# The MLP's gated product split between ScalarE and GpSimd, and VectorE's top-k steps in another order

## The chip, the core and the metric

The kernel runs on one core of one Trainium2 chip. The metric is the device time of one execution in microseconds, the median of several runs.

## What is computed

The input x is 4 batches of 1024 tokens by 256 channels, with a context of 64 tokens and a condition vector for each batch. All of it is float32. Two layers are applied one after the other. The first has three sub-layers, each a layer norm with a scale and shift from the condition, a body, and a gated residual:

```python
h = _ln(x) * (1 + sc_msa) + sh_msa;  h = _self_attn(h, ...);        x = x + h * g_msa
h = _ln(x) * (1 + sc_mca) + sh_mca;  h = _topk_cross_attn(h, ...);  x = x + h * g_mca
h = _ln(x) * (1 + sc_mlp) + sh_mlp;  h = _swiglu(h, ...);           x = x + h * g_mlp

def _swiglu(h, w_m1, b_m1, w_m2, b_m2):
    u = h @ w_m1 + b_m1                     # 256 -> 2048
    a, b = (u[..., :HID], u[..., HID:])     # HID = 1024
    return jax.nn.silu(a) * b @ w_m2 + b_m2
```

The self attention has 16 heads of 16 channels in windows of 128 tokens. The first cross attention keeps for each token and head the 16 largest of 64 scores. The second layer is a plain cross attention with a residual. The change touches how `silu(a) * b` is formed and when the steps of the top 16 run.

## The kernel before

**Blocks and layers.** The 4096 tokens go through in 8 blocks of 512 (two for each batch), each with W = 4 tiles or windows of 128. The code numbers the bodies: layer 1 is the self attention, 2 the top-k cross attention, 3 the MLP, 4 the last cross attention. Work is pipelined over blocks. After `first()` and `second()`, a call `full(a)` for a = 2 to 7 does layer 1 of block a, the scores and the top-k of layer 2 of block c = a - 1, and the rest of layer 2 and layers 3 and 4 of block b = a - 2. `last()` does what is left of blocks 6 and 7, so that it holds two MLPs, and nothing of layer 1. Every engine has its own `full(a)` and `last()`, an order written out by hand; an engine's queue is strictly in this order.

**Banks.** TensorE's results go through the 8 PSUM banks in turn, in the order of `bank_order()`. A result is a key such as ("ua", n, j); TensorE waits until the bank's last user has drained it (`fill_wait`), readers wait until it is filled (`filled_wait`), and the last read is marked with `drain`. So each result needs the one that was 8 places earlier to be read.

**The MLP.** `mlp_in(n)` forms for each of J = 8 chunks j of 128 channels two results of 128x512: "ua" (to be gated by silu) and "ub" (the linear half), six matmuls each: float32 inputs are split in a rounded part and a rest (`qr` and `h_low`; `w_m1` and `m1_low`). Before, ScalarE's `silu(n, j)` (L800 to L805) reads "ua" and writes `sa[:, j % 2, :]`, a buffer of two, which is the tile `rden`. VectorE's `gated_linear(n, j)` (L1074 to L1080) adds the bias to "ub", multiplies by `sa` and writes `hid[:, j, :]` (in the tile `arena`), in one instruction at L1079. `project(3, n)` on TensorE waits until "ub" of chunk 7 is drained and multiplies `hid` by `w_m2`: 64 matmuls, the second MLP product.

**The top-k.** `topk(n, t, steps)` on VectorE (L1042 to L1063) has five steps for a tile t. Steps 0 and 2 find eight maxima of each of 16 heads (L1060), steps 1 and 3 take them out of the scores (L1062), step 4 multiplies the exponentials by the mask (L1054, 128x1024, with two operands in SBUF, `left` and `eS`). Between them GpSimd's `subtract_max(n, t)` (L626 to L631, waits for step 0 of its tile and for step 4 of the tile before) writes `eS`, and ScalarE's `topk_exp(n, t)` (L770) exponentiates it; step 4 waits for that. TensorE's `probs(n)` transposes the result a block later. Exponentials and silu need different tables on ScalarE, so `topk_exp(c, 1)`, which stands in the MLP loop after chunk 3, has a table load on each side.

**Self attention around it.** For window w TensorE forms scores "A" for the maxima. VectorE's `window_max(n, w)` (L1021 to L1026) reduces four banks; TensorE transposes the maxima ("mT") and forms the scores "B" minus the maxima; ScalarE exponentiates them, TensorE forms the values "PV", ScalarE's `self_denominator` (L741 to L750) the reciprocals, and VectorE's `window_divide` (L1028 to L1032) the quotient. In the order of banks the four "B" of window 2 take over the banks of "PV" of window 0 and of the first three "A" of window 3. In `full(a)` before, VectorE runs between `window_max(a, 2)` and `window_max(a, 3)`:

```python
window_max(a, 2)
normalise(4, b, (3, b))
topk(c, 3, (0,))
window_divide(a, 0)
window_max(a, 3)
topk(c, 3, (1,))
```

**GpSimd** has otherwise the reciprocal square roots (`layer_rstd`), the sums `add_bias` (L614) and the scaling of weights by the gates (`gate_weight`, L622). SyncE issues all DMAs.

Of the kernel before, what the change touches and what calls it, by code (L numbers as in the profile page):

```python
# [12 lines left out]
P = 128  # L13
# [12 lines left out]
BT = W * P  # L26
# [221 lines left out]
def build(nc, t_in, out):  # L248
    ctx = ExitStack()
    with ctx:  # L250
# [60 lines left out]
        rden_self = sb("rden_self", [P, 2, KC * P])  # L311
        top = sb("top", [P, H, TOPK])
# [94 lines left out]
        s_rd = [sem(f"cross_denominators{n}") for n in range(5)]  # L407
        s_top8 = sem("top8_done")
# [186 lines left out]
        def _(pool):  # L595
# [29 lines left out]

            def subtract_max(n, t):  # L626
# [29 lines left out]
            for a in range(2, BLOCKS):  # L656
# [7 lines left out]
                if a % BLKS:  # L664
                    gate_weight(1, batch)
                else:
                    gate_weight(0, batch)
                subtract_max(c, 1)
                subtract_max(c, 2)
                layer_rstd(4, b)  # L670
# [10 lines left out]
            add_bias(3, b)  # L681
            subtract_max(c, 1)
            subtract_max(c, 2)
# [4 lines left out]
            add_bias(3, c)  # L688
            layer_rstd(4, c)
# [3 lines left out]
        def _(act):  # L693
# [106 lines left out]
            def silu(n, j):  # L800
                if j >= 2:
                    drained_wait(act, ("ub", n, j - 2))
                key = ("ua", n, j)
                filled_wait(act, key)
                drain(nc.scalar.activation(sa[:, j % 2, :], ps(key), ACT.Silu, bias=chan[:, CB["m1"] + j:CB["m1"] + j + 1]), key)  # L805

# [148 lines left out]
        def _(dve):  # L955
# [118 lines left out]
            def gated_linear(n, j):  # L1074
                drained_wait(dve, ("ua", n, j))
                key = ("ub", n, j)
                filled_wait(dve, key)
                at = CB["m1"] + J + j
                drain(nc.vector.scalar_tensor_tensor(hid[:, j, :], ps(key), chan[:, at:at + 1], sa[:, j % 2, :],  # L1079
                                                     ALU.add, ALU.mult), key)  # L1080

# [144 lines left out]
            def full(a):  # L1226
# [11 lines left out]
                for j in range(J):  # L1238
                    gated_linear(b, j)
                    if j < 5:  # L1240
                        topk(c, 1, (j,))
                    elif j == 5:
                        topk(c, 2, (0,))
                window_max(a, 0)
                window_max(a, 1)
                topk(c, 2, (1, 2))
                residual_moments(3, b, (0,))
                topk(c, 2, (3, 4))
# [3 lines left out]
                topk(c, 3, (0,))  # L1252
                window_divide(a, 0)
                window_max(a, 3)
                topk(c, 3, (1,))
# [12 lines left out]
            def last():  # L1268
# [7 lines left out]
                for j in range(J):  # L1276
                    gated_linear(b, j)
                    if j < 5:
                        topk(c, 1, (j,))
# [520 lines left out]
```

## Time and profile before

| | before |
|---|---|
| median of 3 runs | 1036.91 us (1036.07 to 1039.96) |
| the profiled execution | 1035.79 us, span 1033.6 us |
| TensorE matmul busy | 897.5 us, 87% |
| VectorE busy | 750.6 us, 73%, 3953 instructions |
| ScalarE busy | 475.0 us, 46%, 792 instructions |
| GpSimd busy | 219.1 us, 21%, 162 instructions |
| the chain that ended last | TensorE 58%, VectorE 30%, ScalarE 6%, issue 5% |

Busy time is the time in which an engine has an instruction under way. The chain is followed back from the last instruction, at each step to what released it; "issue" is time in which the engine waited for nothing that the profile shows. TensorE's granted clock, PEclk, is a share of full speed: 1.00 is 2.4 GHz, 0.50 is 1.2 GHz. In the tables below PE is TensorE, DVE is VectorE, ACT is ScalarE and POOL is GpSimd; L1314 and the like are lines of the kernel before. Ends of matmuls are modelled, and all matmuls of one helper share its line, L1314.

### The profile page before, as it was taken

The page shows a single profiled execution, that of the slowest core. Times are in us where ns is not written, and L with a number is a line of the kernel's source. Part 1 is how long each engine was busy: PE and PEld are TensorE (multiplying, and loading weights), DVE is VectorE, ACT ScalarE, POOL GpSimd, SP SyncE. Part 2 cuts the span into 40 slices and gives each one's busy share as a digit, 9 for nine tenths or more (in the row PEclk, how much of TensorE's full clock was granted, in tenths as well). Part 3 has the DMA queues.
Part 4 walks back from the last instruction along what each step waited for, and adds up shares of the span by engine and source line. Part 5 has one row for each costly group of instructions (what it writes and reads, how often), then busy time and mean ns, then how long its engine had stood idle before and what let it go on. Part 6 is the DMA issues. An engine that isn't in the chain of part 4 may idle for free.

```text
span 1033.6 us, 22090 instructions
## 1 busy us (share of the span) xinstructions
PE 897.5 (87%) x8088; PEld 653.4 (63%) x8088; DVE 750.6 (73%) x3953; ACT 475.0 (46%) x792; POOL 219.1 (21%) x162
## 2 busy tenths in 40 slices
PE   6977656998999989998999899998999898767975
PEld 4744543786567756875678656775678566644763
DVE  3647866897579957997589757996599758875322
ACT  3336333625564356526463557426562554315313
POOL 1025411402041404211140404120230303120010
PEclk9988777999999999999999999999999998888999
DMA  8250010000100102000100111000100110000000
GB/s 326 98 168 11 2 42 1 17 2 3 41 17 1 53 18 62 11 2 2 57 2 1 53 50 35 7 2 1 57 2 11 43 31 1 2 1 1 21 1 21
DMA packets 29051, 32.96 MB, mean 32 GB/s; under 512 B 4320, under 2 KB 26000, under 8 KB 28688
## 3 DMA queue, kind: packets, MB, share of 16 engines
q1 hardware_dynamic: 28944, 31.55, 9.4%
q8 instruction: 65, 1.06, 0.4%
q14 instruction: 42, 0.34, 0.1%
HBM read 25.19 MB, written 6.36 MB: 31 GB/s over the span
## 4 chain that ended last, share of the span: by engine, by line
PE 58%; DVE 30%; ACT 6%; issue 5%; DMA 1%; POOL 1%; SPq 0%; DVEq 0%; ACTq 0%; POOLq 0%
PE bank L1314 52%; DVE left L1062 8%; DVE top L1060 6%; DVE negm L1025 3%; DVE arena L1079 3%; PE bank L1481 3%; DVE negm L1087 2%; PE bank L1332 2%; ACT arena L816 2%; DVE arena L1054 1%; DVE xh L973 1%; DVE h_low L1072 1%; ACT hT L705 1%; DVE vpad L1016 1%; DMA w_m<-in_w_ada 1%
## 5 line engine op out<-in xcount | busy, mean ns | idle before, releaser
L1314 PE MATMUL bank<-w_m,arena 128*128 128x256 f32 x512 | 115.2, 387 | 6.1 <-issue 6.1
L601 POOL TENSOR_SCALAR veps<-mv 128x4 f32<-128x4 f32 (+1 forms) x33 | 8.1, 245 | 499.8 <-DVE mv L968 499.7
L1314 PEld LDWEIGHTS bank<-w_m,arena 128*128 128x128 f32 x512 | 98.8, 194 | 20.9 <-issue 6.9
L630 POOL TENSOR_TENSOR eS<-arena,top 128x1024 f32<-128x1024 f32 x32 | 61.9, 1935 | 206.8 <-DVE top L1060 206.7
L1062 DVE MATCH_REPLACE8 left<-top,arena 128x64 f32<-128x64 f32 x512 | 99.8, 208 | 0.0
L1062 DVE MATCH_REPLACE8 left<-top,left 128x64 f32<-128x64 f32 x512 | 99.8, 207 | 0.0
L759 ACT ACTIVATE arena<-bank 128x512 f32<-128x512 f32 x128 | 66.1, 603 | 55.3 <-PE bank L1314 55.3
L805 ACT ACTIVATE rden<-bank,chan 128x512 f32<-128x512 f32 x64 | 44.0, 688 | 102.7 <-PE bank L1314 76.8
L1314 PE MATMUL bank<-qr,w_m 128*128 128x512 f32 x256 | 82.3, 402 | 3.9 <-ACT qr L715 3.2
L1314 PE MATMUL bank<-qr,m_low 128*128 128x512 f32 x256 | 80.4, 396 | 0.0
L1025 DVE TENSOR_REDUCE negm<-bank 128x4 f32<-128x512 f32 x128 | 78.6, 680 | 2.0 <-PE bank L1314 1.9
L1060 DVE MAX8 top<-arena 128x8 f32<-128x64 f32 x512 | 67.7, 209 | 16.2 <-ACT arena L779 16.2
L1314 PE MATMUL bank<-h_low,w_m 128*128 128x512 f32 x256 | 70.3, 396 | 0.5 <-DVE h_low L1072 0.5
L1060 DVE MAX8 top<-left 128x8 f32<-128x64 f32 x512 | 67.8, 209 | 0.5
L999 DVE TENSOR_TENSOR x<-bank,x 128x512 f32<-128x512 f32 x48 | 33.0, 688 | 40.7 <-PE bank L1314 40.7
L724 ACT ACTIVATE qk<-bank,chan 128x512 f32<-128x512 f32 x48 | 33.0, 687 | 63.3 <-PE bank L1314 63.3
L1314 PE MATMUL bank<-q_by_parity,qk 32*128 32x256 f32 x512 | 38.3, 414 | 23.6 <-DVE negm L1025 13.0
L1314 PEld LDWEIGHTS bank<-qr,w_m 128*128 128x128 f32 x256 | 48.6, 191 | 15.8 <-issue 3.6
L1314 PE MATMUL bank<-hT,w_qkv 128*128 128x512 f32 x128 | 58.0, 607 | 0.2 <-ACT hT L705 0.2
L1079 DVE SCALAR_TENSOR_TENSOR arena<-bank,chan,rden 128x512 f32<-128x512 f32 x64 | 46.8, 741 | 15.4 <-ACT rden L805 15.4
L1314 PEld LDWEIGHTS bank<-h_low,w_m 128*128 128x128 f32 x256 | 48.5, 190 | 11.9 <-DVE h_low L1072 1.5
L788 ACT ACTIVATE arena<-bank 128x512 f32<-128x512 f32 x64 | 32.4, 633 | 50.1 <-PE bank L1481 50.1
(133 smaller groups left out, 1840.7 us busy)
## 6 DMA issues: line engine op xcount, KB each, us to landing
w_m<-in_w_m SPq DMA_DIRECT2D x4, 1024.0 KB, 5.5
xin<-in_x SPq DMA_DIRECT2D x4, 512.0 KB, 3.9
arena<-in_w_m SPq DMA_DIRECT2D x1, 2048.0 KB, 12.4
out<-x SPq DMA_DIRECT2D x4, 512.0 KB, 2.9
arena<-in_w_ada SPq DMA_DIRECT2D x1, 1536.0 KB, 10.8
gate<-gate_rows SPq DMA_DIRECT2D x12, 128.0 KB, 3.6
gated_bias<-gate_rows SPq DMA_DIRECT2D x12, 128.0 KB, 3.8
xin<-in_x SPq DMA_DIRECT2D x4, 384.0 KB, 3.1
```

The costliest lines, as they stand in the source:

```text
L630: nc.gpsimd.tensor_tensor(eS[:], S[:, t, :].rearrange("p (h n) -> p h n", h=H), top[:, :, 0:1].to_broadcast([P, H, LC]), ALU.subtract).the ...
L724: drain(nc.scalar.activation(dst, ps(key), ACT.Identity, bias=chan[:, n:n + 1]), key)
L759: drain(nc.scalar.activation(pT_self[:, w % 2, 4 * r:4 * r + 4, :], ps(key).rearrange("p (h q) -> p h q", h=4), ACT.Exp, scale=SCORE_SCALE ...
L788: drain(nc.scalar.activation(pT[:, 4 * k:4 * k + 4, t * P:(t + 1) * P], ps(key).rearrange("p (h q) -> p h q", h=4), ACT.Copy), key)
L805: drain(nc.scalar.activation(sa[:, j % 2, :], ps(key), ACT.Silu, bias=chan[:, CB["m1"] + j:CB["m1"] + j + 1]), key)
L999: drain(nc.vector.tensor_tensor(x[:, slot, tiles], ps(key).rearrange("p (t n) -> p t n", t=2), src, ALU.add), key)
L1025: drain(nc.vector.tensor_reduce(negm[:, w, r, 0:4], ps(key).rearrange("p (h n) -> p h n", h=4), AX_X, ALU.max, negate=True), key)
L1060: i = nc.vector.max(eight, scores)
L1062: i = nc.vector.match_replace(left[:, h, :], eight, scores, REPLACED)
L1079: drain(nc.vector.scalar_tensor_tensor(hid[:, j, :], ps(key), chan[:, at:at + 1], sa[:, j % 2, :], ALU.add, ALU.mult), key)
L1314: return nc.tensor.matmul(dst, lhsT, rhs, start=start, stop=stop)
L1481: i = nc.tensor.transpose(ps(key)[:, p * P:(p + 1) * P], S[:, t, at:at + P], ident[:])
```

## The change

ScalarE's `silu(n, j)` has a second instruction, which copies "ub" with its bias into a new buffer of two, `linear`, and drains it. GpSimd's new `gated(n, first, end)` waits for both and multiplies `sa` and `linear` into `hid`, counted by the new semaphore `s_hid`. `silu` waits for the product two chunks back by `s_hid`, and so does `project(3, n)` for all eight. `gated_linear` goes from VectorE. The products stand in GpSimd's queue around the `subtract_max` of tiles 1 and 2. On VectorE five steps of tile 1 and three of tile 2 run between the last steps of tile 0 and `window_max(a, 0)`, where the gated products and six steps were. Later steps move forward by one or two places. In `last()` it is alike.

```diff
--- before.py
+++ after.py
@@ -309,6 +309,7 @@
         mTs3 = sb("mTs3", [P, BT], F32R)
         rden = sb("rden", [P, 2, BT])
         rden_self = sb("rden_self", [P, 2, KC * P])
+        linear = sb("linear", [P, 2, BT])
         top = sb("top", [P, H, TOPK])
         left = sb("left", [P, H, LC])
         eS = sb("eS", [P, H, LC])
@@ -405,6 +406,7 @@
         s_xb = [sem(f"bias{n}_added") for n in range(5)]
         s_rd1 = sem("self_denominators")
         s_rd = [sem(f"cross_denominators{n}") for n in range(5)]
+        s_hid = sem("mlp_product_done")
         s_top8 = sem("top8_done")
         s_dif = sem("max_subtracted")
         s_exp = sem("topk_exp_done")
@@ -623,6 +625,13 @@
                                                 gate[:].unsqueeze(1).to_broadcast([P, KC, C]), ALU.mult)
                 i.then_inc(s_gated[layer], 1)
 
+            def gated(n, first, end):
+
+                for j in range(first, end):
+                    drained_wait(pool, ("ua", n, j))
+                    drained_wait(pool, ("ub", n, j))
+                    nc.gpsimd.tensor_tensor(hid[:, j, :], sa[:, j % 2, :], linear[:, j % 2, :], ALU.mult).then_inc(s_hid, 1)
+
             def subtract_max(n, t):
                 pool.wait_ge(s_top8, n * W + t + 1)
                 if n + t:
@@ -665,8 +674,11 @@
                     gate_weight(1, batch)
                 else:
                     gate_weight(0, batch)
+                gated(b, 0, 2)
                 subtract_max(c, 1)
+                gated(b, 2, 7)
                 subtract_max(c, 2)
+                gated(b, 7, J)
                 layer_rstd(4, b)
                 add_bias(4, b)
                 subtract_max(c, 3)
@@ -679,13 +691,16 @@
             add_bias(2, c)
             subtract_max(c, 0)
             add_bias(3, b)
+            gated(b, 0, 2)
             subtract_max(c, 1)
+            gated(b, 2, J)
             subtract_max(c, 2)
             layer_rstd(4, b)
             add_bias(4, b)
             subtract_max(c, 3)
             layer_rstd(3, c)
             add_bias(3, c)
+            gated(c, 0, J)
             layer_rstd(4, c)
             add_bias(4, c)
 
@@ -799,10 +814,13 @@
 
             def silu(n, j):
                 if j >= 2:
-                    drained_wait(act, ("ub", n, j - 2))
+                    act.wait_ge(s_hid, n * J + j - 1)
                 key = ("ua", n, j)
                 filled_wait(act, key)
                 drain(nc.scalar.activation(sa[:, j % 2, :], ps(key), ACT.Silu, bias=chan[:, CB["m1"] + j:CB["m1"] + j + 1]), key)
+                key, at = ("ub", n, j), CB["m1"] + J + j
+                filled_wait(act, key)
+                drain(nc.scalar.activation(linear[:, j % 2, :], ps(key), ACT.Identity, bias=chan[:, at:at + 1]), key)
 
             def last_exps(n):
                 pT = probs_of(4, n)
@@ -1070,14 +1088,6 @@
                 for k in range(KC):
                     drained_wait(dve, ("T", 3, n, k))
                     nc.vector.tensor_tensor(h_low[:, k, :], h3T[:, k, :], qr[:, k, :], ALU.subtract).then_inc(s_h_low, 1)
-
-            def gated_linear(n, j):
-                drained_wait(dve, ("ua", n, j))
-                key = ("ub", n, j)
-                filled_wait(dve, key)
-                at = CB["m1"] + J + j
-                drain(nc.vector.scalar_tensor_tensor(hid[:, j, :], ps(key), chan[:, at:at + 1], sa[:, j % 2, :],
-                                                     ALU.add, ALU.mult), key)
 
             def last_max(n):
                 for u in range(2):
@@ -1235,24 +1245,19 @@
                 input_rest(b)
                 take_values(a, 1)
                 topk(c, 0, (3, 4))
-                for j in range(J):
-                    gated_linear(b, j)
-                    if j < 5:
-                        topk(c, 1, (j,))
-                    elif j == 5:
-                        topk(c, 2, (0,))
+                topk(c, 1, (0, 1, 2, 3, 4))
+                topk(c, 2, (0, 1, 2))
                 window_max(a, 0)
                 window_max(a, 1)
-                topk(c, 2, (1, 2))
+                topk(c, 2, (3, 4))
                 residual_moments(3, b, (0,))
-                topk(c, 2, (3, 4))
+                topk(c, 3, (0,))
                 residual_moments(3, b, (1,))
                 window_max(a, 2)
                 normalise(4, b, (3, b))
-                topk(c, 3, (0,))
                 window_divide(a, 0)
+                topk(c, 3, (1,))
                 window_max(a, 3)
-                topk(c, 3, (1,))
                 window_divide(a, 1)
                 last_max(b)
                 topk(c, 3, (2,))
@@ -1273,19 +1278,17 @@
                 topk(c, 0, (0,))
                 input_rest(b)
                 topk(c, 0, (1, 2, 3, 4))
-                for j in range(J):
-                    gated_linear(b, j)
-                    if j < 5:
-                        topk(c, 1, (j,))
-                topk(c, 2, (0, 1))
+                topk(c, 1, (0, 1, 2, 3, 4))
+                topk(c, 2, (0, 1, 2, 3))
                 residual_moments(3, b, (0,))
-                topk(c, 2, (2, 3, 4))
+                topk(c, 2, (4,))
+                topk(c, 3, (0,))
                 residual_moments(3, b, (1,))
-                topk(c, 3, (0,))
+                topk(c, 3, (1,))
                 normalise(4, b, (3, b))
-                topk(c, 3, (1,))
+                topk(c, 3, (2,))
                 last_max(b)
-                topk(c, 3, (2, 3, 4))
+                topk(c, 3, (3, 4))
                 cross_divide(2, c)
                 residual_moments(2, c)
                 cross_divide(4, b)
@@ -1293,8 +1296,6 @@
                 residual(4, b, 0)
                 residual(4, b, 1)
                 input_rest(c)
-                for j in range(J):
-                    gated_linear(c, j)
                 residual_moments(3, c)
                 normalise(4, c, (3, c))
                 last_max(c)
@@ -1422,7 +1423,7 @@
                 if layer == 1:
                     drained_wait(pe, ("PV", n, W - 1))
                 elif layer == 3:
-                    drained_wait(pe, ("ub", n, J - 1))
+                    pe.wait_ge(s_hid, (n + 1) * J)
                 else:
                     drained_wait(pe, ("O", layer, n, KC - 1))
                 for u in range(2):
```

## Rows read from the trace of the kernel before

**Rows 1.** Busy us by stretch (PE, PEld, DVE, ACT, POOL, clock), a = 4.

```profile
390.00:503.00 113.00, 105.93 (x995) 78.20 (x993) 91.17 (x492) 58.25 (x98) 23.39 (x17) 1.00 0.07 20
```

**Rows 2.** TensorE in time, a = 4: start us, us, [idle before <-releaser].

```profile
443.25 1.17 PE L1314 MATMUL bank<-qk,q_by_parity 32*128 32x128 f32 x32 [1.04 <-DVE arena L1079]
...
444.35 14.08 PE L1314 MATMUL bank<-w_m,arena 128*128 128x256 f32 x64
...
469.13 1.10 PE L1314 MATMUL bank<-q_by_parity,qk 32*128 32x256 f32 x13 [1.13 <-DVE negm L1025]
```

**Rows 3.** The chain that ended last: start us, us; three blocks.

```profile
388.12 3.49 PE bank L1481 x32
...
501.09 3.49 PE bank L1481 x32
...
615.19 3.49 PE bank L1481 x32
```

**Rows 4.** Costliest groups: xcount | busy us, mean ns | idle before.

```profile
L630 POOL TENSOR_TENSOR eS<-arena,top 128x1024 f32<-128x1024 f32 x32 | 61.9, 1935 | 206.8 <-DVE top L1060 206.7
...
L1079 DVE SCALAR_TENSOR_TENSOR arena<-bank,chan,rden 128x512 f32<-128x512 f32 x64 | 46.8, 741 | 15.4 <-ACT rden L805 15.4
...
L805 ACT ACTIVATE rden<-bank,chan 128x512 f32<-128x512 f32 x64 | 44.0, 688 | 102.7 <-PE bank L1314 76.8 <-DVE arena L1079 25.8
...
L622 POOL TENSOR_TENSOR w_m<-w_m,gate 128x512 f32<-128x512 f32 x16 | 19.8, 1274 | 0.0
```

**Rows 5.** VectorE in order of time, MLP loop of a = 4.

```profile
423.19 1.23 DVE L1054 SCALAR_TENSOR_TENSOR arena<-left,eS 128x1024 f32<-128x1024 f32 x1
...
424.99 2.11 DVE L1060 MAX8 top<-arena 128x8 f32<-128x64 f32 x16
...
427.02 0.73 DVE L1079 SCALAR_TENSOR_TENSOR arena<-bank,chan,rden 128x512 f32<-128x512 f32 x1
...
430.78 0.74 DVE L1079 SCALAR_TENSOR_TENSOR arena<-bank,chan,rden 128x512 f32<-128x512 f32 x1
...
443.01 4.87 DVE L1025 TENSOR_REDUCE negm<-bank 128x4 f32<-128x512 f32 x8
```

**Rows 6.** ScalarE in order of time, a = 4.

```profile
438.00 0.69 ACT L805 ACTIVATE rden<-bank,chan 128x512 f32<-128x512 f32 x1 [2.06 <-DVE arena L1079]
...
440.75 0.69 ACT L805 ACTIVATE rden<-bank,chan 128x512 f32<-128x512 f32 x1 [2.06 <-PE bank L1314]
...
466.25 0.42 ACT L750 ACTIVATE rden_self<-rden_self 128x256 f32<-128x256 f32 x1
```

**Rows 7.** Two lines of VectorE: duration ns min/median/max.

```profile
L1054 DVE SCALAR_TENSOR_TENSOR arena<-left,eS x32: 1209/1225/1274, 102.4 to 936.5; 128x1024 f32<-128x1024 f32 x32
...
L1072 DVE TENSOR_TENSOR h_low<-xh,qr x16: 680/684/2861, 192.2 to 962.8; 128x512 fp32r<-128x512 f32 x16
```

**Rows 8.** GpSimd in order of time, last stage: a bias sum.

```profile
865.51 2.83 POOL L614 TENSOR_TENSOR x<-x,gated_bias 128x1024 f32<-128x1024 f32 x1
```

**Rows 9.** VectorE in order of time, windows 2, 3 of a = 4.

```profile
461.06 2.48 DVE L1025 TENSOR_REDUCE negm<-bank 128x4 f32<-128x512 f32 x4 [0.25 <-PE bank L1314]
...
463.46 1.37 DVE L973 TENSOR_SCALAR xh<-x,mv,rstd 128x256 f32<-128x256 f32 x4
...
466.79 0.40 DVE L1031 TENSOR_TENSOR oT_self<-bank,rden_self 128x256 f32<-128x256 f32 x1
...
467.11 2.47 DVE L1025 TENSOR_REDUCE negm<-bank 128x4 f32<-128x512 f32 x4
```

**Rows 10.** TensorE in order of time, last stage.

```profile
895.59 16.66 PE L1314 MATMUL bank<-w_m,arena 128*128 128x256 f32 x64 [4.91 <-issue]
...
917.84 2.21 PE L1332 MATMUL bank<-ident,xh 128*128 128x128 f32 x8 [5.59 <-DVE xh L973]
...
984.90 14.05 PE L1314 MATMUL bank<-w_m,arena 128*128 128x256 f32 x64 [1.21 <-issue]
```

**Rows 11.** Busy us and granted clock of a stretch, last stage.

```profile
895.00:897.00 2.00, 1.41 (x3) 1.18 (x4) 2.00 (x14) 1.01 (x1) 0.00 (x0) 0.50 0.00 0
```

## The prediction

> **What bounds the kernel now.** I read the busy time by stage first. In one of the six middle blocks, a = 4, TensorE is busy 105.9 of 113 us and VectorE 91.2; ScalarE has 58.3 and GpSimd 23.4 [rows 1]. So TensorE bounds the middle, and VectorE can only cost time where TensorE stands still for it. Next I read where it stands still [rows 2]: 1.04 us before the second window's scores, where it waits for the last gated product to drain its bank, and 1.13 us before the third window's scores B(a, 2), where it waits for the fourth window's maxima. From 444.35 the second MLP product runs without a hole. The chain of waits passes the block's first transposes every 112.97 us (388.12 to 501.09), and once after 114.10 (501.09 to 615.19) [rows 3]; nothing in a block runs to a clock other than TensorE's own, so what TensorE loses at one place is not given back behind it. Only the last stage, from 842 us on, is sparse enough for VectorE to lead.
>
> **Part 1, the product leaves VectorE.** Removed: 64 gated products of 741 ns, issued 0.65 us apart. Added: 64 ScalarE copies out of PSUM, priced like the silu of the same shape, 688 ns, and 64 GpSimd products. Of those no row exists. Nearest is GpSimd's 128x512 product in place, 1274 ns; its subtraction over 128x1024 takes 1935 ns, which halved gives 0.97, the other end [rows 4]. I take 1.27, the row with the same shape and operation. Per pair of products TensorE needs 2.75 us (438.00 to 440.75 between two silus [rows 6]), ScalarE will need 1.38 and GpSimd 1.27, so neither becomes the bound inside the loop.
>
> VectorE does not get free by it before the maxima. From 423.19 to 443.01 it works without idling [rows 5]. Out go 8 x 0.65 = 5.2 us. In come two top-k steps that used to follow the maxima, tile 2's steps 1 and 2: 3.11 us (430.78 - 427.02 - 0.65) and 2.03 us (427.02 - 424.99), together 5.14. Window 0's maxima start at 443.0 as before.
>
> **Part 2, the lock between VectorE and GpSimd.** New in the change is that GpSimd reads and writes SBUF while VectorE runs step 4 of tile 0 (L1054, two SBUF inputs). So far L1054 never met a GpSimd instruction: its 32 times lie within 1209 to 1274 ns. Another two-input instruction did: L1072 takes 684 ns as a rule and 2861 at worst [rows 7], and that one ran while GpSimd's bias sum was at work from 865.51, itself 2.83 long [rows 8]. The product of j = 0 starts when silu and copy of j = 0 are done, 440.75 - 7 x 2.75 + 0.69 + 0.69 = 422.9, and ends at 424.1 or 424.2; L1054 would start at 423.19 and is held until then, some 0.95 us. Ends: 0 if there is no lock, 1.27 for a whole product. The Trainium skill's "SBUF — State Buffer", section "Who interferes with whom", says that a VectorE instruction with two SBUF inputs and a GpSimd instruction that reads SBUF exclude each other for their full length, while one with a single SBUF input doesn't contend. By that rule the sum has +2.1 us in the next part, without it -1.8.
>
> **Part 3, when the second MLP product starts.** ScalarE finishes the last copy at 440.75 + 1.38 = 442.1 [rows 6], so the second window's scores start some 1.0 us earlier. But the second product now waits for GpSimd: product 6 ends at 438.00 + 1.38 + 1.27 = 440.65, then `subtract_max(c, 2)` stands ahead of product 7 (1.94, to 442.6), then product 7 ends at 443.9. It waits too for the bank of window 0's first maxima, 443.0 + 0.6 = 443.6, with the lock 444.6. Start: 444.0 without the lock, 444.7 with it, against 444.35 [rows 2]: -0.3 or +0.35. I take +0.35, since a two-input row shows the lock: 6 x 0.35 = **+2.1 us**.
>
> **Part 4, the new order of the top-k steps.** This is the largest term. VectorE's work around the fourth window was: maxima of window 2 at 461.06, normalising at 463.46, step 0 of tile 3, division of window 0 at 466.79, maxima of window 3 at 467.11 [rows 9]. The division cannot start before ScalarE's reciprocal is done, 466.25 + 0.42 = 466.67 [rows 6]; step 0 just filled the wait. In the new order step 0 has gone ahead of `residual_moments(3, b, (1,))`, where VectorE has the time. The wait before the division stays empty, though (from the end of the normalising, about 464.8, to 466.7), and step 1, 3.11 us, stands between the division and window 3's maxima. So these start 3.05 us later (3.11 less the 0.06 that the division gains). TensorE needs three of their four banks for B(a, 2), and its queue is in order: last query, values of window 1 and the maxima of layer 4 all stand behind. Its wait goes from 1.13 to 4.2 us. Before, step 1 lay behind the maxima, in a hole in which VectorE waited for TensorE anyway. Price: 6 x 3.05 = **+18.3 us**; ends 2.9 and 3.2 each, since start times move by 0.1.
>
> **Part 5, the clock.** TensorE's granted clock is 1.00 in this block [rows 1]. In the last stage, after 4.91 us of idleness before 895.59, it stands at 0.50 [rows 11], the 1.2 GHz level, and the same 64 matmuls take 16.66 us instead of the 14.05 that they take after 1.21 us of idleness: 2.6 us lost [rows 10]. The block of 114.10 us had one fall without a long wait, 1.1 us lost [rows 3]. A wait of 4.2 us with little work ahead of it lies near the first. I take a fall in five blocks of six at 1.6 us, between 1.1 and 2.6 and nearer the lower since few dense matmuls follow it at once: **+8 us**. Ends: 0 (it never falls) and 6 x 2.6 = 15.6.
>
> **Part 6, the last stage.** In the first of its two MLP products VectorE is behind: TensorE ends at 890.68, the second product starts at 895.59. GpSimd and ScalarE will follow TensorE by 0.69 + 0.27 (the copy has to wait for its silu) + 1.27, so it starts near 893.0. From its end to the next transposes there are 5.59 us now [rows 10]; VectorE comes 1.2 us less late, and step 1 in place of step 0 costs 1.1 more, so 5.4. Transposes: 893.0 + 14.05 + 5.4 = 912.4 against 917.84, a gain of 5.4; if the clock falls in the wait of 2.3 us as well, 2.8. I take the middle, **-4.1 us**. Of the very last MLP product nothing covers the tail: before 984.90 stands a wait of 1.21 for one gated product; now copy and product, one after the other, make it 2.5: **+1.3 us**, with a fall of the clock 3.9. SP's queue moves nowhere; no DMA is added. On GpSimd `layer_rstd(4, b)` stands behind product 7, but the moments it works on come only after the second MLP product's 14 us, so it waits for nothing new.
>
> **Sum.** 2.1 + 18.3 + 8 - 4.1 + 1.3 = +25.6 us on the profiled execution's own 1035.8, so 1061.4 us. The median of the runs shown is 1.1 above the profiled one; a tenth of a per cent.
>
> **Rivals.** (a) *The clock holds* in the waits of 4.2 us. For it: waits around 1 us never lower it. Against: the fall after 4.91 us. Time: 1035.8 + 2.1 + 18.3 - 5.4 + 1.3 = 1052. Chance 0.25. (b) *The clock falls each time* for the full 2.6 and also at the last product: 1035.8 + 2.1 + 18.3 + 15.6 - 2.8 + 3.9 = 1073. Chance 0.15. (c) *Faster: the fourth window's maxima are off the path.* Place: the wait before B(a, 2). If the bank that TensorE waits for there were another's, or if VectorE reached step 1 over 3 us earlier (reciprocal before 464), the 18.3 and the 8 would go, and without the lock the earlier start of part 3 counts: 1035.8 - 1.8 - 5.4 + 1.3 = 1030. It decides for it if window 3's maxima start by 467.2 in this block's time. Against it: TensorE resumes at 469.13, right behind the third of the four maxima, the last that B(a, 2) needs (467.11, 0.6 each). Chance 0.06. (d) *The change doesn't do what it says*: GpSimd, waiting in its queue for the top-k's `s_top8`, holds back silu through the two-deep buffer and so TensorE, inside the loop. In the middle blocks this doesn't reach TensorE: the subtraction of tile 1 ends about 429.3, and the silu that needs product 2 comes at 432 or later. If a whole 1.94 were lost per block on top: 1061.4 + 11.6 = 1073. Chance 0.05. The forecast itself, with a fall in most blocks: 0.49.
>
> **Numbers.** Low: rival (a) with 2.9 for 3.05 and without the lock, 1052 - 0.9 - 3.9 = 1047. High: rivals (b) and (d), 1073. The three runs shown lie 3.9 us apart, so each end moves out by 3, to 1044 and 1076. Outside lie (c) and what (b) and (d) bring together. A measurement of this kernel tells about 0.5% (5 us) from no change. Slower by over 0.5%: forecast, (a), (b), (d), 0.94, less 0.03 for terms that cancel. Faster 0.05, same 0.04, slower 0.91.
>
> **What the profile of after would show.** Right, if TensorE's first B(a, 2) matmul has some 4.2 us of idleness released by L1025, once in each of six blocks, if VectorE idles about 2 us before the division of window 0, if the chain passes a block in 116 to 119 us, and if the clock shows 0.5 shortly after those waits. The lock would show as L1054 at 2 us or so in one of four, the others at 1.23. The second product should start within 0.5 us of where it did. Wrong, if window 3's maxima follow the division at once, if the clock stays 1.00, or if the silus in a middle block space out beyond 2.75 us.

## The result and the profile after

| | before | after |
|---|---|---|
| median | 1036.66 us of 4 runs (1036.07 to 1039.96) | 1074.31 us of 4 runs (1072.76 to 1075.02) |
| the profiled execution | 1035.79 us, span 1033.6 us | 1075.02 us, span 1072.7 us |
| ratio of the medians | | 1.0354, 95% interval 1.033 to 1.0379 |

The changed kernel is 3.5% slower. The forecast was 1061.4 us in a range of 1044 to 1076. So the direction and the range held, and the size came out 13 us short: +25.6 us forecast, +37.7 us by the medians, +39.2 us between the two profiled executions (+39.1 by their spans, which the accounts below use).

First the page of after: the span, the busy time of each engine, and two of the costliest groups (busy us, mean ns | idle before, releaser).

```profile
span 1072.7 us, 22154 instructions
...
PE 912.5 (85%) x8088; PEld 661.4 (62%) x8088; DVE 717.4 (67%) x3889; ACT 511.9 (48%) x856; POOL 307.8 (29%) x226
...
L633 POOL TENSOR_TENSOR arena<-rden,linear 128x512 f32<-128x512 f32 x64 | 89.2, 1399 | 95.0 <-ACT linear L823 93.8
...
L1315 PE MATMUL bank<-q_by_parity,qk 32*128 32x256 f32 x512 | 44.2, 466 | 42.6 <-DVE negm L1043 31.4
```

The totals say that the change did what it was written for: VectorE has 33 us less to do (750.6 before), ScalarE 37 and GpSimd 89 more, and none of the three is near the span. They don't say why the time rose. That stands in the last row: TensorE waited 31.4 us before the scores B for VectorE's maxima. The same row of the page of before has 13.0:

```profile
L1314 PE MATMUL bank<-q_by_parity,qk 32*128 32x256 f32 x512 | 38.3, 414 | 23.6 <-DVE negm L1025 13.0
```

TensorE's matmuls are the same, and yet take 15 us more (897.5 before). Their mean granted clock is 0.944 where it was 0.960.

Next the chain of waits in after, at the first transposes of three middle blocks.

```profile
283.58 3.49 PE bank L1482 x32
...
402.88 3.49 PE bank L1482 x32
...
522.27 3.49 PE bank L1482 x32
```

A block takes 119.3 to 119.5 us; it took 112.97 [rows 3]. Now TensorE in order of time in after: block a = 4 (402.88 here is 388.12 before, so 14.76 is to be taken off), then the last stage.

```profile
455.81 2.29 PE L1315 MATMUL bank<-qk,q_by_parity 32*128 32x128 f32 x64
...
460.12 14.05 PE L1315 MATMUL bank<-w_m,arena 128*128 128x256 f32 x64 [2.02 <-DVE negm L1043]
...
487.90 2.09 PE L1315 MATMUL bank<-q_by_parity,qk 32*128 32x256 f32 x16 [4.16 <-DVE negm L1043]
...
490.67 4.81 PE L1315 MATMUL bank<-hT,w_last 128*128 128x512 f32 x8
...
933.55 15.59 PE L1315 MATMUL bank<-w_m,arena 128*128 128x256 f32 x64 [2.43 <-issue]
...
954.61 2.21 PE L1333 MATMUL bank<-ident,xh 128*128 128x128 f32 x8 [5.47 <-DVE xh L991]
956.83 5.54 PE L1315 MATMUL bank<-hT,w_last 128*128 128x512 f32 x8
...
1023.99 14.05 PE L1315 MATMUL bank<-w_m,arena 128*128 128x256 f32 x64 [2.41 <-issue]
```

The second product starts at 445.36 in before's time, 1.0 us late against [rows 2]. B(a, 2) starts at 473.14, 4.0 us late, after a wait of 4.16 us where it was 1.13. Its own 16 matmuls then take 2.09 us and not 1.10. The block gains 6.42 us in all, so another 2.4 us come in behind the wait. The windows of 2 us around it show from what (PE, PEld, DVE, ACT, POOL busy, then the granted clock):

```profile
484.00:486.00 2.00, 0.00 (x0) 0.00 (x0) 2.00 (x22) 0.85 (x3) 0.84 (x1) 1.00 0.00 0
486.00:488.00 2.00, 0.10 (x4) 0.13 (x4) 2.00 (x4) 0.00 (x0) 0.00 (x0) 0.53 0.00 0
488.00:490.00 2.00, 2.00 (x24) 1.81 (x26) 0.35 (x1) 0.00 (x0) 0.00 (x0) 0.50 0.00 0
490.00:492.00 2.00, 2.00 (x18) 1.36 (x15) 0.00 (x0) 1.27 (x3) 0.00 (x0) 0.50 0.00 0
492.00:494.00 2.00, 2.00 (x4) 0.74 (x4) 0.00 (x0) 0.79 (x2) 0.00 (x0) 0.77 0.00 0
```

The clock goes to half (1.2 GHz) within the wait, some 1.8 us before B starts, and TensorE's first 5 us of work behind it run at that level.

VectorE in order of time in after, the same block and one row of the last stage:

```profile
437.95 2.08 DVE L1072 SCALAR_TENSOR_TENSOR arena<-left,eS 128x1024 f32<-128x1024 f32 x1
...
439.96 2.10 DVE L1078 MAX8 top<-arena 128x8 f32<-128x64 f32 x16
...
445.33 2.12 DVE L1078 MAX8 top<-left 128x8 f32<-128x64 f32 x16
...
459.30 4.86 DVE L1043 TENSOR_REDUCE negm<-bank 128x4 f32<-128x512 f32 x8
...
482.44 0.42 DVE L1049 TENSOR_TENSOR oT_self<-bank,rden_self 128x256 f32<-128x256 f32 x1 [1.95 <-ACT rden_self L765]
...
485.89 2.47 DVE L1043 TENSOR_REDUCE negm<-bank 128x4 f32<-128x512 f32 x4
...
929.73 2.33 DVE L1072 SCALAR_TENSOR_TENSOR arena<-left,eS 128x1024 f32<-128x1024 f32 x1
```

The division waits 1.95 us, which step 0 of tile 3 used to fill, and step 1 fills the 3.03 us between its end and window 3's maxima. In [rows 9] these begin 0.3 us after the division begins. GpSimd in the same block:

```profile
437.64 1.31 POOL L633 TENSOR_TENSOR arena<-rden,linear 128x512 f32<-128x512 f32 x1 [5.96 <-ACT linear L823]
...
454.57 1.32 POOL L633 TENSOR_TENSOR arena<-rden,linear 128x512 f32<-128x512 f32 x1 [0.16 <-ACT linear L823]
455.85 1.93 POOL L639 TENSOR_TENSOR eS<-arena,top 128x1024 f32<-128x1024 f32 x1
457.74 1.29 POOL L633 TENSOR_TENSOR arena<-rden,linear 128x512 f32<-128x512 f32 x1
```

The first product ends at 438.95, and step 4, started by the profile at 437.95, comes out at 2.08 us where it took 1.23 [rows 5].

The account of the spans' 39.1 us: the six middle blocks +40.0, the start -0.7, the last stage -0.2. In the blocks, 18.5 us of added wait before B (3.03 to 3.20 each), six times 1.0 at the second product (6.0), 14.2 of half clock behind B (some 2.4 each), one more fall in a second product of 15.69 us (1.6), less the fall of 1.1 us that before had in one block. The last 0.8 is not explained; it lies in the first of the six blocks, whose second product came 2.15 us late and not 1.0.

### The profile page after: what moved, and what is told of

Read it like the earlier page. It is cut to its first block, busy times and chain, and to the rows that moved or that the text cites. A ratio compares the mean times of both kernels' runs of the same rounds, so it can differ in the third digit from the quotient of the medians.

```text
span 1072.7 us, 22154 instructions
## 1 busy us (share of the span) xinstructions
PE 912.5 (85%) x8088; PEld 661.4 (62%) x8088; DVE 717.4 (67%) x3889; ACT 511.9 (48%) x856; POOL 307.8 (29%) x226
## 4 chain that ended last, share of the span: by engine, by line
PE 58%; DVE 28%; ACT 8%; issue 3%; DMA 1%; POOL 1%; SPq 0%; DVEq 0%; ACTq 0%; POOLq 0%
PE bank L1315 54%; DVE left L1080 11%; DVE top L1078 6%; ACT arena L774 2%; DVE negm L1043 2%; PE bank L1482 2%; DVE negm L1097 2%; DVE arena L1072 2%; PE bank L1333 2%; ACT arena L834 2%; ACT hT L720 1%; DVE h_low L1090 1%; DVE vpad L1034 1%; DVE oT_self L1049 1%; ACT rden_self L765 1%
## 5 line engine op out<-in xcount | busy, mean ns | idle before, releaser
L633 POOL TENSOR_TENSOR arena<-rden,linear 128x512 f32<-128x512 f32 x64 | 89.2, 1399 | 95.0 <-ACT linear L823 93.8
L774 ACT ACTIVATE arena<-bank 128x512 f32<-128x512 f32 x128 | 66.1, 602 | 81.7 <-PE bank L1315 81.7
L1049 DVE TENSOR_TENSOR oT_self<-bank,rden_self 128x256 f32<-128x256 f32 x32 | 13.4, 419 | 103.0 <-ACT rden_self L765 103.0
L1315 PE MATMUL bank<-q_by_parity,qk 32*128 32x256 f32 x512 | 44.2, 466 | 42.6 <-DVE negm L1043 31.4
L770 ACT ACTIVATE mTs<-bank 128x128 fp32r<-128x128 f32 x32 | 9.0, 282 | 106.4 <-PE bank L1384 106.4
L1315 PEld LDWEIGHTS bank<-q_by_parity,qk 32*128 32x128 f32 x512 | 28.5, 218 | 49.7 <-issue 48.3
```

The lines of the kernel that those rows point to most:

```text
L633: nc.gpsimd.tensor_tensor(hid[:, j, :], sa[:, j % 2, :], linear[:, j % 2, :], ALU.mult).then_inc(s_hid, 1)
L774: drain(nc.scalar.activation(pT_self[:, w % 2, 4 * r:4 * r + 4, :], ps(key).rearrange("p (h q) -> p h q", h=4), ACT.Exp, scale=SCORE_SCALE ...
L1049: drain(nc.vector.tensor_tensor(oT_self[:, :, w * P:(w + 1) * P], ps(key)[:, 0:KC * P].rearrange("p (c n) -> p c n", c=KC), rden_self[:, w ...
L1315: return nc.tensor.matmul(dst, lhsT, rhs, start=start, stop=stop)
```

## The experiments

Theory T: the position of step 1 ahead of window 3's maxima costs most, directly and through the clock. Rivals: the split itself, or the lock between VectorE and GpSimd. Each ratio is against runs of the kernel before on the same chip; their medians were 1037.36, 1040.52, 1040.34 and 1040.40 us in the four groups.

**The maxima first.** The changed kernel with one pair of lines in their old order.

```diff
                 window_divide(a, 0)
-                topk(c, 3, (1,))
                 window_max(a, 3)
+                topk(c, 3, (1,))
```

> The kernel after, with one exchange in full(a) on VectorE: the fourth window's maxima run ahead of step 1 of tile 3 again; the product split and all else stay. Theory (the order is the cost): TensorE's wait before B(a, 2) falls from 4.16 to about 1.1 us and the clock no longer falls there, so six times 3.0 + 2.4 = 32.6 us come back and the time is about 1042. Rival (the split itself is the cost, through ScalarE, GpSimd or the lock): the time stays above 1065.

1047.29 us (1045.53 to 1048.61), ratio 1.0096 (1.0068 to 1.0124). Against the changed kernel 27 us are back, from one line. TensorE in time:

```profile
334.96 15.64 PE L1315 MATMUL bank<-w_m,arena 128*128 128x256 f32 x64 [2.04 <-DVE negm L1043]
...
361.23 1.10 PE L1315 MATMUL bank<-q_by_parity,qk 32*128 32x256 f32 x13 [1.03 <-DVE negm L1043]
```

The wait before B is 1.03 to 1.07 in all six blocks. What stays are the waits of 2.04 us before the second product, and in this block the clock was low behind it (15.64 for 14.05). That happened in two of the six blocks. In three blocks the clock also fell some 43 us after the second product's start, at the scores of the last layer, for 1.1 us each; before had one such fall (its block of 114.10). Blocks take 113.9 to 116.7 us. The expectation was 5 us low for these falls, which come to 6.5 us where the changed kernel had one of 1.6 outside the place before B.

**The split alone.** The changed kernel with all of VectorE's top-k steps where they stood before, less the gated products.

```diff
-                topk(c, 2, (0, 1, 2))
+                topk(c, 2, (0,))
                 window_max(a, 0)
                 window_max(a, 1)
-                topk(c, 2, (3, 4))
+                topk(c, 2, (1, 2))
                 residual_moments(3, b, (0,))
-                topk(c, 3, (0,))
+                topk(c, 2, (3, 4))
                 residual_moments(3, b, (1,))
                 window_max(a, 2)
                 normalise(4, b, (3, b))
+                topk(c, 3, (0,))
                 window_divide(a, 0)
-                topk(c, 3, (1,))
                 window_max(a, 3)
+                topk(c, 3, (1,))
```

The steps of the last stage go back in the same way.

> The kernel after, but VectorE runs the order of the kernel before with the gated products left out (five steps of tile 1 and one of tile 2, then the maxima, and so on; last() alike). Theory: window 0's maxima come 5 us earlier and no longer hold the second MLP product; it starts when GpSimd's last product is done, which is where it started before. Middle blocks 113.0 us as before, the last stage 0 to 3 us shorter: 1034 to 1037. Rival (the split costs by itself): above 1042.

1037.79 us (1035.01 to 1039.64), ratio 0.9999 (0.9986 to 1.0013): no difference. TensorE in time:

```profile
331.44 14.05 PE L1315 MATMUL bank<-w_m,arena 128*128 128x256 f32 x64 [1.03 <-issue]
...
356.13 1.10 PE L1315 MATMUL bank<-q_by_parity,qk 32*128 32x256 f32 x13 [0.86 <-DVE negm L1043]
```

Moving the product costs nothing and brings nothing. VectorE stands idle for 3.0 us ahead of the first maxima, and TensorE now waits 1.03 us for GpSimd's product 7, behind the subtraction. All the loss lies in the order of VectorE's steps, or in that order together with the split.

**The order alone.** The kernel before, gated products on VectorE, with one pair of lines swapped.

```diff
                 window_divide(a, 0)
-                window_max(a, 3)
                 topk(c, 3, (1,))
+                window_max(a, 3)
```

> The kernel before, gated product on VectorE, with one exchange in full(a): step 1 of tile 3 ahead of the fourth window's maxima. Theory: TensorE waits 4.2 us before B(a, 2) and its clock falls each time; six times 3.1 + 2.4 = 33 us on top of before, about 1070. Rival (the step costs only together with the split): within 5 us of before, 1037 to 1042. If only the wait and not the clock counts: 1055.

1072.55 us (1071.31 to 1074.69), ratio 1.0341 (1.0315 to 1.0366). TensorE in time:

```profile
485.89 2.09 PE L1314 MATMUL bank<-q_by_parity,qk 32*128 32x256 f32 x16 [4.22 <-DVE negm L1025]
```

The wait is 4.22, 3.61, 4.22, 4.22, 4.21 and 4.17 us in the six blocks. One swapped pair of lines in the kernel before gives nearly the whole loss of the change. Blocks take 117.7 to 119.4 us: some 3.1 us of added wait cost 4.7 to 6.4, on average 5.8.

**The lock taken away.** The changed kernel, with GpSimd's first product held until step 4 of tile 0 is over.

```diff
+                pool.wait_ge(s_prob, c * W + 1)
                 gated(b, 0, 2)
```

> The kernel after, with a wait on GpSimd ahead of the first two products in full(a) until step 4 of tile 0 is done, so that the two no longer meet. Theory (lock): VectorE's step 4 of tile 0 goes from 2.08 back to 1.23 us, window 0's maxima and with them the second MLP product start 0.85 us earlier, six times: 1069. Rival (the 2.08 us have another reason): the step still takes 2.08 and the time stays at 1074. If the later products hold ScalarE back: above 1075.

1073.18 us (1072.80 to 1074.32), ratio 1.0346 (1.0324 to 1.0369); the changed kernel stands at 1074.31. VectorE, then TensorE, in time:

```profile
435.74 1.23 DVE L1073 SCALAR_TENSOR_TENSOR arena<-left,eS 128x1024 f32<-128x1024 f32 x1
```

```profile
457.07 14.05 PE L1316 MATMUL bank<-w_m,arena 128*128 128x256 f32 x64 [1.19 <-DVE negm L1044]
...
484.93 2.09 PE L1316 MATMUL bank<-q_by_parity,qk 32*128 32x256 f32 x16 [4.17 <-DVE negm L1044]
```

The lock is real: without GpSimd at work the step takes 1.23 us again, and the wait before the second product shrinks from 2.02 to 1.19. The 5 us that this should give are mostly missing. In five of the six blocks the chain gains 0.1 to 0.7 us each (118.6 to 119.4 for 119.3 to 119.5); the first gains 3.1, with one fall of the clock fewer and a shorter one. B(a, 2) comes 0.75 us sooner in this block, but the stretch from B(a, 2) to the next transposes (519.75 in this kernel's chain) is 34.8 us here and 34.4 in the changed kernel. The very last MLP product, too, ran with a fallen clock, 15.74 us for 14.05. In windows of 2 us the clock of this kernel falls some 0.9 us before B starts, and that of the changed kernel 1.8 us before, so here more of TensorE's work runs at half. So in these profiles a gain ahead of the wait was partly given back by the clock behind it.

**A part of the step ahead.** The kernel before, with 8 or 4 of the 16 heads of step 1 ahead of the maxima. These set the length of the wait.

```diff
                 window_divide(a, 0)
+                topk_part(c, 3, range(8), False)
                 window_max(a, 3)
-                topk(c, 3, (1,))
+                topk_part(c, 3, range(8, H), True)
```

> The kernel before, with half of step 1 of tile 3 (8 of 16 heads) ahead of the fourth window's maxima and the rest behind. The wait before B(a, 2) should be 1.07 + 1.55 = 2.6 us. If only the wait costs: six times 1.55 = 9 us, 1046. If the clock falls after such a wait as it did after 4.2 us: six times 1.55 + 2.4, 24 us, 1061. With a fall in some blocks: between the two.

> The kernel before, with 4 of 16 heads of step 1 of tile 3 ahead of the fourth window's maxima. The wait before B(a, 2) should be 1.07 + 0.78 = 1.85 us. If the price is the wait alone: six times 0.78 = 4.7 us, 1042. If the clock falls here too: 1056.

Eight heads: 1060.97 us (1055.79 to 1062.31), ratio 1.0183 (1.0146 to 1.0221). Four heads: 1052.85 us (1047.71 to 1054.45), ratio 1.011 (1.0078 to 1.0143). Windows of the kernel with eight heads, around a wait of 2.69 us that ends at 482.62:

```profile
482.00:484.00 2.00, 1.38 (x27) 1.41 (x28) 2.00 (x13) 0.00 (x0) 0.00 (x0) 0.88 0.04 8
484.00:486.00 2.00, 2.00 (x14) 1.27 (x12) 0.63 (x7) 1.44 (x3) 0.00 (x0) 0.50 0.00 0
486.00:488.00 2.00, 2.00 (x5) 0.74 (x4) 0.00 (x0) 0.63 (x2) 0.00 (x0) 0.76 0.00 0
```

With eight heads (waits 2.58 to 2.69) the clock fell in six blocks of six; here it falls after the wait, when TensorE is already at work. With four (2.04, 1.32, 1.92, 1.52, 1.84 and 1.89) it fell in four of six, each time for some 1.65 us (10.8 us to the next scores, for 9.15). In this place a wait under 2 us is already not safe.

**The wait filled.** The swapped kernel of before, with extra matmuls into B(a, 2)'s first bank while TensorE would stand still; their results are overwritten. This parts the wait from the clock.

```diff
+                if w == 2 and n >= 2:
+                    spare = ("B", n, w, 0)
+                    fill_wait(pe, spare)
+                    for _ in range(15):
+                        mm(ps(spare)[:, 0:C], w_qkv[:, 0, 0:P], w_qkv[:, 1, 0:C], True, True)
                 for r in range(RG):
                     fill_wait(pe, ("B", n, w, r))
```

> order_alone (step 1 of tile 3 ahead of the fourth window's maxima, gated product on VectorE), with 15 extra 128x256 matmuls, 3.3 us, in TensorE's wait before B(a, 2); their results are overwritten and nothing else changes. Theory (part of the price is the clock): the clock stays at 1.00 there, the wait itself costs 3.1 us in each of six blocks and the rest comes back: 1037 + 19 = 1056, against 1072.6. Rival (the whole price is the wait and what hangs on it): no change from 1072.6.

1076.14 us (1074.11 to 1079.03), ratio 1.0357 (1.0327 to 1.0386). A miss in its size: TensorE in time shows that the 15 matmuls ran as 30 and took 6.6 us.

```profile
482.63 6.64 PE L1314 MATMUL bank<-w_qkv 128*128 128x256 f32 x30
```

So they filled more than the wait and TensorE itself came late, by 5.3 us at B. The clock stayed at 1.00 around it, but in five of the six blocks it fell some 18 us later, at the scores of the last layer, behind waits of 0.69 and 0.76 us:

```profile
508.00:510.00 2.00, 2.00 (x16) 0.28 (x12) 1.97 (x14) 1.15 (x3) 0.00 (x0) 0.50 0.00 0
```

That fall cost 1.1 us a block, so blocks take 119.2 to 119.4 us, and this run doesn't part the two prices. The same with 8 matmuls:

> As wait_filled, but with 8 extra matmuls instead of 15. In wait_filled each of them ran as two of 0.22 us, so that 15 filled 6.6 us of a wait of 4.2 and TensorE came 2.4 us late; 8 fill 3.5 us and should end before the maxima release B(a, 2). Theory (wait and clock each have a share): six times 3.1 us of wait remain, the clock holds there, time 1056 to 1060. Rival (all is the wait): as order_alone, 1072.

1055.77 us (1052.66 to 1061.96), ratio 1.0165 (1.0129 to 1.0201). TensorE in time, then the window:

```profile
473.58 3.62 PE L1314 MATMUL bank<-w_qkv 128*128 128x256 f32 x16
...
477.98 1.10 PE L1314 MATMUL bank<-q_by_parity,qk 32*128 32x256 f32 x13 [0.78 <-DVE negm L1025]
```

```profile
476.00:478.00 2.00, 1.22 (x9) 0.77 (x8) 2.00 (x5) 0.00 (x0) 0.00 (x0) 1.00 0.00 0
```

B starts no earlier for it, since VectorE is as late as before, and still the kernel with more work is 17 us faster than the one that stands still (1072.55). In all six blocks the clock holds. The chain passes a block in 116.06 us, 3.1 more than before: that is the wait alone. The swapped kernel's blocks take another 1.6 to 3.3 us, on average 2.7: the half clock. This parts the two terms of the forecast.

**Can the split pay?** On the split with the old order: GpSimd's last product ahead of the subtraction of tile 2.

```diff
-                gated(b, 2, 7)
+                gated(b, 2, J)
                 subtract_max(c, 2)
-                gated(b, 7, J)
```

> The split alone (VectorE's order of before without the gated products), and on GpSimd the last product ahead of subtract_max of tile 2. Theory: what holds the second MLP product is GpSimd's queue (the subtraction, 1.9 us, ahead of product 7); without it the wait of 1.04 us shrinks to about 0.1 and six blocks lose 0.9 us each: 1032. Rival (the copy and the product themselves are too long for it): no change, 1037.

1038.38 us (1033.01 to 1041.73), ratio 0.9987 (0.9966 to 1.0007). The wait before the second product falls from 1.03 to 0.21 or 0.22 us and a block takes 112.2 us (113.35 where the clock fell once), but the median is 6 us above the expected 1032. The profiled execution lost 5 us in its start:

```profile
102.35 5.82 DVE L1071 SCALAR_TENSOR_TENSOR arena<-left,eS 128x1024 f32<-128x1024 f32 x1
```

That is step 4 of the first tile, 1.3 us in most of the other profiles. With that change, and the last block's gated product back on VectorE (the wait of 2.4 us before the very last product is bare, since nothing lies beside it):

```diff
             add_bias(3, c)
-            gated(c, 0, J)
...
                 input_rest(c)
+                for j in range(J):
+                    gated_linear(c, j)
```

> As product_first, but the MLP of the last block has its gated product on VectorE as in the kernel before, where VectorE has nothing else to do. Theory: the wait before the very last second MLP product goes from 2.4 back to 1.2 us: 1.2 us less than product_first, more if the clock fell there. If the tail of copy and product is hidden: no difference.

1030.91 us (1029.19 to 1035.31), ratio 0.9911 (0.9885 to 0.9936): 0.9% below the kernel before, clear of its interval, and 7.5 us below the run above, for an expected 1.2. TensorE in time:

```profile
330.69 14.05 PE L1328 MATMUL bank<-w_m,arena 128*128 128x256 f32 x64 [0.21 <-issue]
...
890.34 14.05 PE L1328 MATMUL bank<-w_m,arena 128*128 128x256 f32 x64 [3.80 <-issue]
...
978.09 14.05 PE L1328 MATMUL bank<-w_m,arena 128*128 128x256 f32 x64 [1.21 <-issue]
```

Of the 6.2 us between the spans (1033.6 and 1027.4), 2.6 lie ahead of the last stage, which its chain reaches at 838.50 and before's at 841.11, and 3.6 in it: VectorE is less late for the first of the two MLPs there, and that product ran at full clock behind a wait of 3.80 us, in 14.05 us for the 16.66 of before. These 2.6 us are the clock. The fastest kernel of the next group has the same order; there the clock did fall (15.74 us behind 3.18) and its last stage was as short (188.4 us; this one 188.9, before 192.5). How much of the 3.6 is luck stays open, as the last stage of the split alone took 3.4 us longer than before's.

**The lock at the start.** Step 4 at some 102 us met GpSimd's two `m1_low` subtractions and took 1.2 to 1.3 us or 5.8 to 5.9 (three profiles: this one and those with eight and four heads ahead). Both kernels, with GpSimd held until the step is over:

```diff
             pool.wait_ge(s_m1_round, KC)
+            pool.wait_ge(s_prob, 1)
             for k in range(KC):
```

> last_on_vector with one more wait on GpSimd: the subtractions that split w_m1 (128x2048, two of some 5 us) start only when VectorE's first step 4 (L1054 of before) is done. In the runs so far that step, which starts around 102 us, took 1.3 us in some profiles and 5.8 in others, whichever of the two engines came first. Theory (a lock that either may win): the step takes 1.2 us each time, the slow start is gone, and the runs lie close together, at 1029 to 1032. Rival (the scatter has another cause): the runs spread over 6 us or more as before.

> The kernel before with the same wait. Theory: its runs no longer spread over 8 us but over 3 or less, at 1034 to 1037. Rival: the median rises by what the subtractions start later, about 1 us per subtraction that a product waits for, and the spread stays.

The fastest kernel with it: 1030.42 us (1028.33 to 1034.02), ratio 0.9922 (0.9897 to 0.9946). The kernel before with it: 1038.02 us (1034.75 to 1041.58), ratio 0.9987 (0.9969 to 1.0005). The runs of the plain kernel spread over 8.7 us in that group and with the wait over 6.8, and the fastest kernel's over 5.7 with the wait and 6.1 without. The expectation of 3 us or less was wrong: this lock can be at most a part of the scatter, and what the rest is stays open. The wait itself brought nothing beyond the intervals (0.9922 against 0.9911, and 0.9987 with 1 inside its interval).

## Why the prediction was right, and where its sizes were off

By the spans the terms missed 13.5 us, and nearly all in one direction: 3.9 in part 3, 0.2 in part 4, 6.2 in part 5 and 1.6 for a fall in a second product, 2.6 in part 6, and 0.8 unexplained; less 1.1 for the fall that before had and 0.7 at the start. So the range held by its upper end, which came from rivals (b) and (d) and the 3 us of scatter, and not by the forecast's own case. Two of its signs failed: a block takes 119.3 to 119.5 us, for 116 to 119, and the second product starts 1.0 us late, for 0.5 at most.

**Part 1, durations.** ScalarE's copy took 0.68 us (0.69 forecast). GpSimd's product has a median of 1.31 (1.27 forecast; the mean of 1.40 holds those that met step 4). TensorE stays dense in the MLP loop, and no engine became a bound there.

**Part 2, the lock.** Shown: 2.08 us for step 4 of tile 0 where the forecast had 0.95 + 1.23 = 2.18, and 1.23 with GpSimd held back. By the Trainium skill's "SBUF — State Buffer", section "Who interferes with whom", the two exclude each other for their full length; this case's rows agree, and the 5.82 us at the start are one GpSimd instruction of some 4.6 us waited for, and 1.2 of its own.

**Part 3, the second product.** Mis-sized: +1.0 us for +0.35. The lock was there at the forecast size, so the rest is something that the step left out. VectorE's six top-k steps now follow one another directly. The first lasts 5.37 us with its neighbour (439.96 to 445.33) where the steps with gated products between came to 2.03 + 3.11 = 5.14 [rows 5]: some 0.12 us for each. By the code a step within a tile waits for a semaphore of the one before. In after such a step starts 0.03 us behind the end of the last instruction, while step 0 of the next tile, which has no such wait, starts 0.08 us ahead of that end, as every instruction of before's loop did: the wait used to lie under the gated product. Six such steps make 0.7. VectorE's stretch from step 4 to the maxima is 21.35 us for 19.82. The forecast for TensorE had the right releaser (window 0's maxima), and in one block the clock fell in that wait too.

**Part 4, the order.** Right, and the largest term: a wait of 4.16, 4.14, 4.16, 4.16, 4.16 and 4.16 us for a forecast of 4.2; 18.5 us for 18.3. The one swapped pair gives it in the old kernel and takes it away in the new.

**Part 5, the clock.** The mechanism was right, its size was not, and this is the main error: 14.2 us, a fall in six blocks of six at some 2.4, for 8 us, five falls at 1.6. The forecast took a value between 1.1 and 2.6, near the lower end, because few dense matmuls follow. The row nearest in cause, a fall after a long wait (2.6 [rows 10]), was the better price than the row without a wait (1.1 [rows 3]): what follows B here keeps TensorE busy without a hole for the 5 us of half clock, whatever the form of its matmuls, and the loss is about half of them. With 8 matmuls in the wait the clock held in all six blocks, and the cost was gone.

**Part 6, the last stage.** Mis-sized: -0.2 us for -2.8. The forecast gain at the first second product is there in part: its wait shrank from 4.91 to 2.43, but it starts only 1.36 us sooner, counted from the stage's start, for 2.6 forecast, since the stage's first transposes stood still for 1.2 us (VectorE waited 5.0 us for a store of `x` and not 3.2). It took 15.59 us for 16.66 [rows 10], so the next transposes come 2.55 us sooner. But the clock was low again when the last queries came, 5.54 us for 4.32 at the same 8 matmuls, and the bare tail of the very last product cost the forecast 1.2 (2.41 for 1.21). The gain was spent by the time the stage ended.

**Rivals.** (a), the clock holds, is refuted: it fell in six blocks of six. (b), it falls each time, at a chance of 0.15, was nearest, with 1073, for the reason it named; its 2.6 us a block are 2.4, and at the very last product it did not fall in this profile. (a) also said that waits around 1 us never lower the clock; they did at the scores of the last layer. (c), the maxima are off the path, is refuted by the maxima first and the order alone. Its case that the split could be faster by itself holds only after two more edits, at 0.991. (d): GpSimd's subtraction held nothing back in the loop.

## What to carry to other kernels

Time freed on an engine that is not the bound is worth nothing by itself, and an instruction moved into it costs its full length where the bounding engine's releaser stands behind: go through the order around each release (here maxima, division, maxima), not through the totals. A wait of TensorE has two prices, its length and the half clock behind it; here 3.1 us of added wait brought another 2.4 us of half clock on average in the changed kernel and 2.7 with the order alone. A cheap test for such a suspicion is to swap the one pair of lines in the old kernel, and to fill the wait with idle work, no longer than the wait, to see what the clock alone is worth.

## What the runs showed of the hardware that was not expected

- In front of B the clock fell at waits of 1.52, 1.89, 1.92 and 2.04 us and held at 1.32 and 1.84; at 2.6 us it fell in all six blocks, and before, at 0.94 to 1.13 us, in none.
- The length of a wait does not decide alone. Behind 2.0 us before the second product it fell in one block of six (the changed kernel) and two of six (the maxima first). Behind 2.4 us before the very last product it fell in some profiles (15.74 us) and not in others (14.05). In the last stage of the fastest kernel it held behind 3.80 us.
- At the scores of the last layer, behind waits of 0.69 and 0.77 us, the clock fell in one block of before, three with the maxima first and five with 15 matmuls in the wait, for 1.1 us each.
- 8 useless matmuls in a wait made a kernel 17 us faster (1055.77 for 1072.55), by keeping the clock up.
- One VectorE instruction, step 4 at 102 us, lasts 1.2 or 5.8 us by whether GpSimd's second subtraction of 4.6 us has started first.
- A float32 matmul of 128x256 shows as two passes of 0.22 us each (15 issued, 30 in the row). So the 64 matmuls in the rows of a second product are 32 in the code.
- A VectorE step that waits for the one before starts 0.03 us behind its end, one that doesn't wait starts 0.08 us ahead of it: 0.12 us for each dependent step.
